# Layer three's MLP: its weights split during its attention, its first norm and products inside the last items

## What is computed

```python
def _forward(x, xf_1, xf_2, ...):            # third layer
    h = _layer_norm(x, ln1_scale, ln1_offset)
    x = x + _cross_attention(h, xf_1, wq1, ..., bias_k1, bias_v1)
    h = _layer_norm(x, ln2_scale, ln2_offset)
    x = x + _cross_attention(h, xf_2, wq2, ..., bias_k2, bias_v2)
    h = _layer_norm(x, ln_mlp_scale, ln_mlp_offset)
    h = gelu(h @ w_fc1 + b_fc1, approximate=False) @ w_fc2 + b_fc2
    return x + h
```

## Time and profile before

| | us |
|---|---|
| median of 3 runs (lowest, highest) | 2182.54 (2181.51, 2183.78) |
| profiled execution | 2176.38 |
| its span | 2174.6 |
| PE busy in the span | 1944.5 (89%) |
| DVE, ACT, POOL busy | 1074.2, 955.5, 690.8 |

### The profile page before, as it was taken

One profiled execution on the slowest core, in us unless ns is written; L12 is line 12 of the kernel. 1 busy time (PEld: TensorE's weight loads), 2 busy tenths in 40 slices (PEclk: granted clock), 3 DMA queues, 4 the chain that ended last, 5 costly groups with the idle time before them and its releaser, 6 DMA issues.

```text
span 2174.6 us, 39268 instructions
## 1 busy us (share of the span) xinstructions
PE 1944.5 (89%) x16109; PEld 1652.2 (76%) x16109; DVE 1074.2 (49%) x1954; ACT 955.5 (44%) x2550; POOL 690.8 (32%) x803
## 2 busy tenths in 40 slices
PE   6788887898999999999999999999879778878798
PEld 4566665787888888888788888888766656756687
DVE  3444554544444444455454444444363577677743
ACT  4244334343434444334333444434334467666633
POOL 3322222411322313233233231321131267667500
PEclk9999998999999999999999999999989899999899
DMA  3000000100000000000010010000020100000000
GB/s 106 10 7 7 2 21 21 54 1 20 20 20 9 31 1 20 11 1 20 11 38 22 7 34 1 11 1 1 2 88 1 49 2 2 7 1 6 2 16 24
DMA packets 27747, 38.45 MB, mean 18 GB/s; under 512 B 1312, under 2 KB 19376, under 8 KB 27568
## 3 DMA queue, kind: packets, MB, share of 16 engines
q1 hardware_dynamic: 27568, 35.95, 5.1%
HBM read 33.84 MB, written 2.10 MB: 17 GB/s over the span
## 4 chain that ended last, share of the span: by engine, by line
PE 77%; DVE 10%; ACT 8%; issue 3%; POOL 2%; DMA 1%; SPq 0%; DVEq 0%; ACTq 0%; POOLq 0%
PE ps_high L195 41%; PE ps_four L195 7%; PE ps_four L2510 5%; PE ps_four L2530 5%; PE ps_four L2519 3%; PE ps_four L2314 2%; PE ps_high L2406 2%; ACT l_pt L1645 2%; PE ps_high L2297 1%; PE ps_four L2322 1%; PE ps_high L2335 1%; DVE l_sm L2062 1%; PE ps_four L2446 1%; POOL l_sm L1499 1%; PE ps_four L2436 1%
## 5 line engine op out<-in xcount | busy, mean ns | idle before, releaser
L1741 ACT ACTIVATE l_prob<-ps_four,l_mx 128x129 f32<-128x129 f32 x512 | 181.3, 367 | 574.9 <-DVE l_mx L2097 574.9
L1533 POOL TENSOR_TENSOR l_prob<-l_prob,l_mx 128x516 f32<-128x516 f32 x128 | 134.1, 1048 | 753.4 <-DVE l_mx L2104 753.4
L195 PE MATMUL ps_high<-ctxT,l_wk 128*128 128x512 f32 x768 | 215.1, 416 | 0.0
L195 PEld LDWEIGHTS ps_high<-l_wo,l_ao 128*128 128x128 f32 x1536 | 199.2, 190 | 17.7 <-DVE l_ao L2116 6.8
L195 PE MATMUL ps_high<-l_wo,l_ao 128*128 128x256 f32 x1536 | 205.5, 283 | 5.5 <-DVE l_ao L2116 5.5
L195 PE MATMUL ps_high<-l_hT,l_wq 128*128 128x512 f32 x768 | 209.6, 408 | 0.0
L195 PE MATMUL ps_high<-l_wv,ctxT 128*128 128x512 f32 x768 | 204.6, 402 | 1.6 <-ACT l_qT L1722 1.3
L1499 POOL TENSOR_TENSOR l_sm<-l_sm,l_mask 128x1024 f32<-128x1024 f32 x64 | 150.3, 2371 | 120.5 <-DVE l_sm L2062 120.4
L195 PEld LDWEIGHTS ps_high<-l_wv,ctxT 128*128 128x128 f32 x768 | 144.0, 191 | 44.9 <-ACT l_qT L1722 9.8
L195 PEld LDWEIGHTS ps_high<-ctxT,l_wk 128*128 128x128 f32 x768 | 138.2, 193 | 24.0
L2116 DVE SCALAR_TENSOR_TENSOR l_ao<-ps_four,columns,l_ao 128x512 fp32r<-128x512 f32 x128 | 96.2, 751 | 116.8 <-ACT l_ao L1751 116.8
(11 more groups left out here) (285 smaller groups left out, 3862.9 us busy)
## 6 DMA issues: line engine op xcount, KB each, us to landing
l_staging<-in_L_xattn_wv SPq DMA_DIRECT2D x8, 512.0 KB, 4.0
l_staging<-in_L_xattn_wk SPq DMA_DIRECT2D x8, 512.0 KB, 3.8
l_staging<-in_L_xattn_wq SPq DMA_DIRECT2D x8, 512.0 KB, 4.2
l_staging<-in_L_xattn_wo SPq DMA_DIRECT2D x8, 512.0 KB, 3.6
ctx_tok<-in_ctx SPq DMA_DIRECT2D x8, 256.0 KB, 3.3
x_tok<-in_x SPq DMA_DIRECT2D x4, 512.0 KB, 5.6
l_raw_w<-in_L_xattn_mlp_w SPq DMA_DIRECT2D x2, 1024.0 KB, 7.3
l_w<-in_L_xattn_w_fc SPq DMA_DIRECT2D x2, 1024.0 KB, 6.3
```

The costliest lines, as they stand in the source:

```text
L195: ins = e.matmul(out, a, b, start=start and i == 0, stop=stop and i == 2, skip_group_check=not check)
L1533: e.tensor_tensor(pr[:, :, 0:S + 1], pr[:, :, 0:S + 1], mx[:, 3, :].unsqueeze(2).to_broadcast([P, GB, S + 1]), ALU.mult).then_inc(sem("poo ...
L1741: ins = e.activation(pr.t[:, b, 0:S + 1], banks[b // 2].t[:, (b % 2) * (S + 2):(b % 2) * (S + 2) + S + 1], ACT.Exp, bias=mx[:, 1, b:b + 1] ...
```

## The change

The weights of layer three's MLP are loaded and split like one more set of the attention's: four parts of 512 KB into the attention's staging ring, each split on POOL in two halves (`m_w`), one step for each attention step from 119 on. Its tiles (`mhs`, two hidden tiles, both weights) lie where the hidden states of groups 0 and 1 and the first weight set of the attention were, and wait for their last readers; `l2_space` and `l2_space_too` are unused bytes that move addresses. The first group's norm runs as a chain in `norms_ahead` from step 118, with the attention's transposing banks and staging tiles, and writes the split input directly. `mlp2(0)` gives four of its steps in each of the steps 128 and 129, in banks 6, 7, 0, 1 (`within`), and the rest behind the barrier, in the same banks. The attention loop is a step shorter (step N + 2 emitted nothing, N = 128); the rate of the side chain beside `mlp2(0)` is 8.0 instead of 5.0; SP begins with `l3_loads`, and the weights of `l3e` are loaded behind them without a wait.

```diff
-L3_MLP2_SLACK, L3_MLP2_RATES = 12, (5.0, 9.5, 9.5)
+L3_MLP2_SLACK, L3_MLP2_RATES = 12, (8.0, 9.5, 9.5)
...
+        items = [...]
+        with ExitStack() as mlp_scope:
+            weights_read = ("pe.l2_out", end_of(1, 2, 3, 3))
+            self.mlp_tiles("l2m", mlp_scope, (("full", "l2_q", end_of(1, 3, 1, 3)), ("full", "l2_q", end_of(1, 3, 0, 3)),
+                                              weights_read, weights_read))
+        self.l2m_tiles, self.hid3 = (self.mhs, self.hid3), hid
...
+        def load_mlp_weights():
+            for name, part in (("w1", 0), ("w2", 0), ("w1", 1), ("w2", 1)):
+                yield from pl.until(staging)
+                pl.slot(staging, "l2_staging", "l2m", name, part)
+                i = staging.slots.index(pl.use["l2_staging", "l2m", name, part].slot)
+                pl.emit("m_w_load", name, part, landed=self.dma(f"sp.l2_staging{i}"))
+                for half in range(2):
+                    yield
+                    pl.emit("m_w", name, part, half)
+                pl.free("l2_staging", "l2m", name, part, by=("pool.m_w", name, part, 1))
+
+        def first_mlp():
+            t = ("l2m", 0)
+            pl.slot(self.mhs, "mhs", t)
+            def add_bias():
+                self.x_done[0] = self.bias_rows(t, 0, self.l2m_b2, (self.norms[t]["xn_stage"], t, 1))
+            self.l2m_first = yield from self.norm(t, 0, None, self.x_done[0], self.cols("L2_xattn_ln_mlp_scale"),
+                                                  self.cols("L2_xattn_ln_mlp_offset"), False, 1e-5, ("mhs", t), add_bias)
...
+                if last and at == 1 and g == 0:
+                    norms_ahead.append(first_mlp())
...
+            if g == 1 and h == 0 and nxt[0] == 2:
+                weights_ahead.append(load_mlp_weights())
...
-        for step in range(N + 3):
+        self.mhs, self.hid3 = self.l2m_tiles
+        mlp = self.l2m_mlp = self.within(self.mlp2(0), self.banks(6, 7, 0, 1), self.work, self.st, self.xn_stage)
+        for step in range(N + 2):
             ...
             if 2 <= step <= N + 1:
                 values(step - 2)
+            if step >= N:
+                next(mlp)
+                next(mlp)
             advance(weights_ahead, 1)
             ...
             if 2 <= step <= N + 1:
                 output(step - 2)
+            if step >= N:
+                next(mlp)
+                next(mlp)
             if 1 <= step <= N:
                 transposes(step - 1)
         self.barrier("l3")
...
-        pl.emit("l2m_loads")
         pl.emit("l3_loads")
+        pl.emit("l3_mlp_loads")
...
-        with ExitStack() as mlp_scope:
-            self.mlp_tiles("l2m", mlp_scope, (None,) * 4)
-            self.xn_stage = "dve.norm_xn"
-            first, weights = norm2(0), self.mlp_weights("l2m", ("sp.l2m_plain", 32))
-            for stages, n in ((first, 7), (weights, 1), (first, 1000), (weights, 2)):
-                for _ in range(n):
-                    next(stages, None)
-            self.slack = L3_MLP2_SLACK
-            interleave(mlp2(0), chain(weights, norm2(1), self.load_weight("l3_w_kv", ...)), L3_MLP2_RATES[0])
+        self.xn_stage = "dve.norm_xn"
+        self.slack = L3_MLP2_SLACK
+        interleave(self.l2m_mlp, chain(norm2(1), self.load_weight("l3_w_kv", ...)), L3_MLP2_RATES[0])
...
-        pl.emit("l3_mlp_loads", after=last)
...
+        def m_w(name, part, half):
+            ...
+            e.tensor_scalar(hi, st, 1.0, 1.0, ALU.mult, ALU.mult).then_inc(sem("pool.m_w:hi"), 1)
+            q.wait_ge(*pl.done("pool.m_w:hi", name, part, half))
+            e.tensor_tensor(lo, st, f32(hi), ALU.subtract).then_inc(sem("pool.m_w"), 1)
```

More of the change, by code:

```diff
@@ L786, in plan_l2_attention @@
         late = [s for k in (PT, AO, pbT, hT[0], QT, KT, PR) for s in k.slots]
[L787 to L792, removed]
+        hT2 = Ring([Slot(sb("l2_hT2", [P, 2, DC, T], F32R))])
         MX = self.ring("l2_mx", 2, [P, 4, GB], F32, scope)
@@ L795, in plan_l2_attention @@
         self.BW, self.dv, self.dsel = sb("l2_bw", [H2, D]), sb("l2_dv", [P, H2]), sb("l2_dsel", [P, 2, H2, H2], F32R)
+        sb("l2_space", [P, L2_SPACE[0]])
+        V = Ring([Slot(sb("l2_V0", [P, GB, HG * K2]))])
+        staging = self.ring("l2_staging", 3, [P, DC * HG * K2], F32, scope)
+        self.xn = self.ntmp = self.staging = staging
+        V = Ring([*V.slots, Slot(sb("l2_V1", [P, GB, HG * K2]))])
+        self.l2_bo = [sb(f"l2_bo{i}", [P, D]) for i in (1, 2)]
+        sb("l2_space_too", [P, L2_SPACE[1]])
+        items = [(at, hg, g, h) for at in range(2) for hg in range(H2 // HG) for g in range(G) for h in range(HG)]
+        self.items = items
+        N, hid = len(items), self.hid3
+        end_of = lambda *item: items.index(item)
+        with ExitStack() as mlp_scope:
[3 more added lines that the diff above has]
+        self.l2m_tiles, self.hid3 = (self.mhs, self.hid3), hid
+        hT = [*(Ring([Slot(sb(f"l2_hT{g}", [P, 2, DC, T], F32R))]) for g in (1, 0)), hT2, hT[0]]
+        hT = [hT[1], hT[0], hT[2], hT[3]]
+        W = {k: Ring([Slot(sb(f"l2_{k}0", s, F32R)), second[k]]) for k, s in shapes.items()}
         self.st = self.norm_tiles("l2a", scope)
@@ L974, in plan_l2_attention, with mlp2 @@
         self.barrier("l3")
+    def mlp2(self, g):
+        t = ("l2m", g)
+        yield from self.mlp_split(t, "l2m", self.cols("L2_xattn_b_fc1"), ACT.Gelu, None if g else self.l2m_first)
+        self.x_done[g] = self.x_add(t, g, t, self.x_done[g])
     def plan_l3(self, scope):
@@ L1100, in norm2 @@
             yield from self.mlp_input(("hs", t), t, h_done[t])
[L1102 to L1106, removed]
         def norm3(g):
@@ L1330, in l2_w_load, with m_w_load @@
             e.dma_start(dst, src).then_inc(sem(pl.info["l2_w_load", k, at, hg]["landed"][1]), 16)
-        def l2m_loads():
-            for n, t in (("w_fc1", "w1"), ("w_fc2", "w2")):
-                e.dma_start(self.l3_w[t][:], a["L2_xattn_" + n].rearrange("(c p) n -> p c n", p=P)).then_inc(sem("sp.l2m_plain"), 16)
-            e.dma_start(self.l2m_b2[:], a["L2_xattn_b_fc2"].partition_broadcast(P)).then_inc(sem("sp.l2m_bias"), 16)
+        def m_w_load(name, part):
+            u = use["l2_staging", "l2m", name, part]
+            q.wait_ge(*pl.event(u.before))
+            if name == "w1":
+                src = a["L2_xattn_w_fc1"].rearrange("(c p) n -> p c n", p=P)[:, :, part * F // 2:(part + 1) * F // 2]
+            else:
+                src = a["L2_xattn_w_fc2"].rearrange("(c p) n -> p c n", p=P)[:, part * FC // 2:(part + 1) * FC // 2, :]
+            e.dma_start(u.t[:].rearrange("p (c n) -> p c n", c=src.shape[1]), src).then_inc(
+                sem(pl.info["m_w_load", name, part]["landed"][1]), 16)
         def l3_loads():
```

59 lines of the change are left out of this document (35 added, 24 removed).

## The result

| | median | lowest to highest | executions | span of the profiled one |
|---|---|---|---|---|
| before | 2182.06 us | 2181.12 to 2183.78 | 6 | 2174.6 us |
| after | 2171.72 us | 2168.22 to 2173.73 | 6 | 2171.1 us |

A forecast was written before the change was run, and what follows sets the result against it. TensorE bounds the kernel except at the attention-MLP border, where it waits and runs at half clock. 16.9 - 4.7 - 1.6 - 0.6 - 1.5 = 8.5 us gained: 2182.54 to 2174.0, likeliest 2171 to 2177, eight in ten 2169 to 2180.5.

The forecast's parts named there:

- Up 5 earlier by 16.9 us: Border of attention and MLP: group 0's sixth up product starts at 1586.2 instead of 1603.06, despite three PE waits.
- The norm costs 4.7 us: Attention: carrying the first norm from item 120 on adds 4.7 us, between 3.7 and 6.7.
- Splits on POOL cost nothing: Items 119 to 127: eight half weight splits on POOL cost 0, at most 15 us.
- Second norm 1.6, clock 1.5: Group 1's norm behind the barrier loses 1.6 us; half clock after three PE waits costs 1.5, range 0 to 5.
- Late `w_kv` 0.6: Layer four's weights land later, so DVE waits for POOL at the next norm: 0.6 us, range 0 to 3.
- The paragraph on the shared ports: Side sum: VectorE and GpSimd lock each other's ports; the later split could cost 2.4 us instead of 0.6.
- Moved tiles and pads "cost nothing that a row shows": Moved tiles and `l2_space` pads change addresses, not waits: 0 us.
- The price of group 1's wait: Behind the barrier, PE waits 1.1 to 2.0 us for the second norm on DVE, where the old wait was 0.5.
- the gap doesn't go: Rival, chance 0.03: products ahead of the barrier run at their latency, up 5 comes at 1595; gain 2 us, 2180.5.
- Behind layer four's first group "the order of work is the old one": From there on nothing changes but earlier MLP load issue, so the gain carries through whole.
- Rivals with a dear clock or a POOL-bound attention: Half clock after all three waits, 5 us, 2177.5, chance 0.1; POOL splits delay eight items, 15 us, 2187.5, chance 0.05.
- The prediction's own sign of being wrong: Wrong if split items exceed 8.1 us, the barrier comes over 30 us behind last scores, or layer four loses the gain.

The follow-up runs named there:

- `norm_bank2`: Changed kernel with products in the last two steps reordered to avoid three waits, and the first norm's transposes in bank 2 alone; ratio to before 0.9918.
- `before_layout`: Kernel before with all the change's tile moves and pads in layers two and three, nothing else; ratios to before 1.0 and 0.9987.
- `ring_turned`: Changed kernel with layer four's ring of eight banks begun at bank 5; ratio to before 0.9942.
- `after_again`: Changed kernel unchanged, run and profiled a second time; ratio to before 0.9959.

## Why the prediction was right, step by step

- **Up 5 earlier by 16.9 us.** Right. Behind the last scores it comes at 27.3 us (forecast 27.7, before 44.5): 17.2 us gained. The waits measured 2.28, 2.21 and 2.16 us for 2.4, 2.2 and 2.4, at the named places with the named releasers.
- **The norm costs 4.7 us.** Right: item 120 takes 13.17 us for 7.97, 5.2 more; items 119 to 123 together 5.1 more. The clock's mean was 0.87, as in item 61's row. In `norm_bank2`, at full clock and in another bank, the norm costs 3.3.
- **Splits on POOL cost nothing.** Right: item 121 took 7.81 us, in the forecast's 7.8 to 8.1, PE full.
- **Second norm 1.6, clock 1.5.** Their sum was right, not the split: from up 5 to group 1's up 0 it took 18.3 us, 3.2 more than before, and the half clock came only here, behind the barrier; neither of the first two waits was followed by it. The forecast for this stretch alone, 16 to 17.5, was too low, as it had put the clock in front of it.
- **Late `w_kv` 0.6.** The term that was mis-sized. `w_kv` landed 18.1 us behind the barrier, 1 later than forecast, at 1610.77, but the price was not DVE's wait for POOL at the next norm. It was DVE blocked by POOL in front of a hidden tile: 0.88, 2.98 and 2.63 us of PE in three executions. With the ring's 1.54 us this makes 2.4 and 4.5 of the 3.0 and 5.1 us measured, for a forecast of 0.6. The paragraph on the shared ports had the mechanism, and priced it at 2 us more, but the sum left it out.
- **Moved tiles and pads "cost nothing that a row shows".** Wrong: the attention is 4.0 us shorter, and `before_layout` has that without any other part of the change. By themselves the moves gain nothing, as its border is 3.8 us longer.
- **Slips in the working.** The price of group 1's wait, "1.1 to 2.0", comes to 0.9 to 1.8 from its own terms (3.9 to 4.8 of DVE less 3.0 of PE). In the rival "the gap doesn't go", up 5 at 1595 instead of 1603.06 is 8 us and not 9. Neither moves the forecast by more than 0.2 us.
- **Behind layer four's first group "the order of work is the old one".** The order is, the banks are not: the turned ring costs 1.54 us before the first scores (`ring_turned` takes it away).

The gain of the border itself, 8.8 to 9.3 us for a forecast of 9.1, is the mechanism foreseen, and it came. That the whole came out within 2.3 us is in part luck: two misses stood against each other, -4.0 in the attention and +2.4 to +4.5 behind the border (3.0 and 5.1 measured, 0.6 forecast). Rivals with a dear clock or a POOL-bound attention did not occur. The prediction's own sign of being wrong, that what is gained at the border is lost again in layer four, came true for a third to a half of it.

Open: which property of an operand's address makes the product 3% faster; what decides how long the clock is at half in the start; why the old border with the new layout has 34.1 us of half clock. Not run: `norm_bank2` with the `ring_turned` edit alone.

## What to carry to other kernels

Work moved ahead of a barrier pays by the latencies it exposes there: the first placing of the products was worth nothing net, and the same products reordered gained 4 us (2170.72 to 2166.84, run in turn), so check what stands in front of each in-order queue, and in which bank. After an edit to tile allocation compare the untouched stages first, at equal time at half clock; a stage of the same instructions may change by its addresses. A transfer made to land earlier brings its POOL work earlier, and the place to look is what DVE has to do for PE at that moment.

## What the runs showed of the hardware

- A chain of twelve output matmuls takes 1.425 us or 1.375 with its operands at other SBUF addresses, with PE full and the clock at 1.00 in both; V products of six matmuls of 512 columns 1.39 or 1.365.
- POOL's split and memset hold up some of DVE's instructions, small ones too: 128x2 `TENSOR_SCALAR` x4 took 7.22 us instead of 0.61, a cast 3.30 (beside the memset) instead of 0.42, and 6.04 (beside subtraction and memset). An instruction that waits can wait through several of POOL's in a row, and what stands behind it in DVE's queue waits too: the hidden tile's subtraction, which reads PSUM, took 2.92 us behind it in `after_again`. Not held up are a subtraction from PSUM (0.69 us beside POOL's subtraction) and `BATCH_NORM_STATS2` (0.41 each beside the memset), both in `norm_bank2`. The Trainium skill (SBUF — State Buffer, Who interferes with whom) says that a cast or a tensor_scalar in a two-port mode and GpSimd exclude each other for a whole instruction; the runs agree for the cast and the tensor_scalar, and show that this holds at two columns; the 5.93 us of one tensor_scalar are longer than any single instruction of POOL there (2.40).
- Where the half clock lies is in part a property of the program: two profiles of one layout both have 34.1 us of it at the border, against 23.9 and 20.5 in two of the kernel before. In part it is the execution's: the same two profiles have 17.1 and 10.2 us of it between item 0 and item 119.
